# A decoder layer whose shared expert moves from first to last in the feed-forward order

## The chip, the core and the metric

The kernel runs on one core of a Trainium2 chip. A core has five engines with queues of their own: TensorE (PE in the profile, its weight loads PEld), VectorE (DVE), ScalarE (ACT), GpSimd (POOL) and SyncE (SP, which here only starts transfers). They meet through semaphores that the program sets and waits for. The metric is the device time of one execution in microseconds (us). Smaller is better.

## The reference, cut to what matters

One decoder layer on 8 sequences of 56 tokens and 128 channels: self-attention with 16 heads, attention over a context of 1500 rows by random features, and a feed-forward part with one shared expert and eight routed experts. Each part is added to its input. The change touches the feed-forward part:

```python
def _L0_ffn_ref(x, W_router, W_up, W_down, W_sh_up, W_sh_down):
    logits = x_flat @ W_router
    probs = jax.nn.sigmoid(logits)
    topk_probs, topk_idx = jax.lax.top_k(probs, TOPK)
    topk_probs = topk_probs / (jnp.sum(topk_probs, axis=-1, keepdims=True) + 1e-06)
    combine = jnp.zeros((N, E), dtype=x.dtype).at[jnp.arange(N)[:, None], topk_idx].add(topk_probs)
    out = sq_relu(x_flat @ W_sh_up) @ W_sh_down
    for e in range(E):
        h = sq_relu(x_flat @ W_up[e])
        out = out + combine[:, e:e + 1] * (h @ W_down[e])
```

All eight routed experts are computed for all 448 tokens; the combine weights are zero for those that a token did not choose. Each expert has 512 hidden columns, and `sq_relu` is the square of the positive part.

## The kernel before, in words

The program is written out by hand, one list of instructions for each engine; nothing reorders them. The 8 sequences go as 4 pairs (`PAIRS`). The attention of a pair and the context products of two sequences alternate up to 64 us of the profiled execution. From there the last pair's second half (residual, norm, context attention, norm) is a chain of small steps across four engines, into which TensorE puts feed-forward products of the first three pairs. After that only feed-forward work is left.

The hidden columns of the nine experts are 36 chunks of 128 (`NCH`), `c` = 0 to 35, four to an expert. Before, chunks 0 to 3 are the shared expert and chunks 32 to 35 the last routed one. The first 32 (`NSP`) are computed with each operand split into a high half in float32r and a low half, three products for each result: high by high, low weights by high, high weights by low. The last four are plain float32 products. For each chunk:

- TensorE makes the up product (`up`, 3 matmuls of 448 columns) into one of five banks, five chunks ahead of the down product (`down`, 3 more) into one of the output banks, of which before has two (C0, K0), in turn by expert.
- ScalarE takes the positive part (`relu`), and later the high half of the squared result (`hidden_high`, to `hh`); for some early chunks it also squares (`square`). VectorE squares the others (`hidden`).
- The low half `hl` is the square less `hh` (`hidden_low`): GpSimd does it for chunks with `on_pool(c)`, VectorE for the others. The down product of a chunk ends with the one that reads `hl`.
- When an expert's four down products are there, VectorE multiplies the bank by the expert's row of combine weights (`expert_out`), and GpSimd adds the product to the running sum `acc` (`add_expert`).

The combine weights go a long way: router products for each pair (`router`), exponent on ScalarE, `choose_probs` to `choose_weights` on VectorE, four small transposes on TensorE into X0, a copy to `cT` on ScalarE, a write to memory (`share`) by SyncE and reads of it that spread each expert's row over 128 partitions (`cb`). `s_cb[0]` counts the first two rows, `s_cb[1]` the rest.

The down weights arrive in six pieces of six chunks (`weights(k)`, k = 6 to 11), ScalarE takes their high halves (`weights_high`) and GpSimd their low ones (`weights_low`). For the late pieces the tables `LATE_AT` and `LOW_AT` say after which chunk each is done. On GpSimd, then, low halves of the hidden values, low halves of weights and the additions of experts stand in one queue. At chunk c it does `hidden_low(c)`, then `add_expert` (where c ends an expert), then `weights_low`.

At the end the last chunk's products stand in C0, the sum `acc` is transposed into X0, VectorE adds X0 to the residual `x2` (`base`), then multiplies C0 by the last expert's combine weight and adds, a pair at a time (`fin`, four operations). Two transfers of two pairs each leave from SyncE's and ScalarE's queues. `keep_warm(n)` is n float32 products of 128 columns with no use but to keep TensorE busy.

## Time and profile before

| | us |
|---|---|
| Runs of the kernel | 126.13 median (124.91, 126.13, 127.34) |
| The profiled execution's own time | 124.76 |
| Its span, first to last instruction | 123.0 |
| TensorE busy | 113.9 (93%) |
| VectorE busy | 89.6 (73%) |
| ScalarE busy | 75.8 (62%) |
| GpSimd busy | 59.1 (48%) |

Busy times overlap between engines. The share of TensorE counts every matmul from its start to its modelled end, so neighbours overlap; where only one stage matters, start-to-start distances are the ones to read. The profiled execution lies below all three timed runs. Feed-forward work fills the stretch from about 72.5 us to 119.5 us.

### The profile page before, as it was taken

The numbers are of one execution on the slowest core, as the hardware profiler recorded it, in microseconds if no ns is written. First come the engines' busy times: TensorE is split into PE (matmuls) and PEld (weight loads), VectorE is DVE, ScalarE is ACT, GpSimd is POOL, SyncE is SP. The second block draws the span as 40 slices with busy tenths as digits, with TensorE's granted clock in tenths as the row PEclk, the third lists the DMA queues.
The fourth block names the chain that finished last, engine by engine and source line by source line (L and its number), as shares of the span: only waits on it lengthen the run. The fifth ranks groups of instructions, "written<-read, shape, count | busy, mean of one in ns | idle before, by whom it ended". The sixth has DMA issues, their size and how long they took to land.

```text
span 123.0 us, 3129 instructions
## 1 busy us (share of the span) xinstructions
PE 113.9 (93%) x1171; PEld 91.1 (74%) x1171; DVE 89.6 (73%) x241; ACT 75.8 (62%) x167; POOL 59.1 (48%) x65
## 2 busy tenths in 40 slices
PE   3989999999999999999996969999999999999980
PEld 2357757686869676776674859989998999999980
DVE  0679898227969686967664469999579999999442
ACT  4013527983677566871941766999768988986300
POOL 6397242351965289251011041637957794673110
PEclk9999999999999999999999996799999999999999
DMA  3899999769969995992000000032892000000002
GB/s 117 236 316 374 406 426 392 248 247 290 351 185 424 344 419 142 418 347 80 0 5 0 0 3 0 5 53 87 241 303 101 3 0 0 5 0 0 0 0 85
DMA packets 6198, 20.46 MB, mean 166 GB/s; under 512 B 776, under 2 KB 2344, under 8 KB 6184
## 3 DMA queue, kind: packets, MB, share of 16 engines
q1 hardware_dynamic: 6040, 20.14, 46.3%
q8 instruction: 9, 0.15, 0.5%
q10 hardware_dynamic: 144, 0.13, 0.3%
q14 instruction: 5, 0.04, 0.1%
HBM read 19.99 MB, written 0.28 MB: 165 GB/s over the span
## 4 chain that ended last, share of the span: by engine, by line
PE 85%; DVE 6%; POOL 4%; issue 2%; ACT 1%; DVEq 0%; POOLq 0%
PE RA L378 6%; PE K L304 5%; PE C L293 5%; PE K L440 3%; PE C L556 3%; PE C L646 3%; PE C L553 3%; PE RA L331 3%; PE C L552 3%; PE K L556 3%; PE K L552 3%; PE K L553 3%; PE RA L552 3%; PE M L402 3%; PE RA L556 3%; PE RB L388 2%
## 5 line engine op out<-in xcount | busy, mean ns | idle before, releaser
L881 POOL TENSOR_TENSOR hl<-craw,hh 128x448 fp32r<-128x448 f32 (+2 forms) x12 | 12.9, 1073 | 12.8 <-ACT hh L799 12.8
L845 POOL TENSOR_TENSOR rstd<-vpe,mhalf 128x1 f32<-128x1 f32 (+1 forms) x10 | 5.8, 583 | 23.5 <-DVE vpe L980 23.5
L881 POOL TENSOR_TENSOR wul<-wraw,wuh 128x768 fp32r<-128x768 f32 x6 | 10.9, 1822 | 8.4 <-ACT wuh L693 8.4
L881 POOL TENSOR_TENSOR wdl<-wraw,wdh 128x768 fp32r<-128x768 f32 (+1 forms) x6 | 9.9, 1653 | 3.3 <-ACT wdh L693 3.3
L926 POOL TENSOR_TENSOR kT<-kT,qT 128x448 f32<-128x448 f32 x7 | 8.1, 1152 | 5.8 <-DVE qT L1261 5.8
L785 ACT ACTIVATE rt<-RA 128x448 f32<-128x448 f32 (+2 forms) x17 | 8.5, 498 | 1.2 <-PE RA L556 0.9
L799 ACT ACTIVATE hh<-craw 128x448 fp32r<-128x448 f32 (+2 forms) x16 | 7.9, 503 | 1.3 <-DVE craw L1222 1.2
L785 ACT ACTIVATE rt<-RB 128x448 f32<-128x448 f32 (+2 forms) x15 | 7.7, 517 | 0.7 <-PE RB L556 0.7
L378 PEld LDWEIGHTS RA<-kT,qT 64*64 64x64 f32 x256 | 7.1, 134 | 0.8 <-issue 0.8
L378 PE MATMUL RA<-kT,qT 64*64 64x56 f32 x256 | 7.6, 221 | 0.0
L965 DVE STREAM_TRANSPOSE rft<-rf 128x384 f32<-128x384 f32 x8 | 4.6, 575 | 3.5 <-ACT rf L684 3.4
L293 PE MATMUL C<-craw,pk 128*32 128x384 f32 x64 | 6.7, 492 | 0.4 <-ACT rf L684 0.4
L304 PE MATMUL K<-craw,rft 128*32 128x129 f32 x192 | 6.9, 277 | 0.0
L556 PE MATMUL C<-hl,wdh 128*128 128x448 f32 (+2 forms) x19 | 6.9, 365 | 0.0
L553 PE MATMUL C<-hh,wdl 128*128 128x448 f32 (+2 forms) x19 | 6.8, 360 | 0.0
L552 PE MATMUL C<-hh,wdh 128*128 128x448 f32 (+2 forms) x19 | 6.7, 352 | 0.0
L552 PE MATMUL RA<-y3h,wuh 128*128 128x448 f32 (+2 forms) x17 | 6.4, 377 | 0.0
L873 POOL TENSOR_TENSOR ktok<-rt 128x256 f32<-128x256 f32 x8 | 5.7, 730 | 1.4 <-DVE rt L1035 1.4
L684 ACT ACTIVATE rf<-C 128x384 f32<-128x384 f32 x8 | 3.9, 490 | 3.5 <-PE C L293 3.3
L553 PE MATMUL RA<-y3h,wul 128*128 128x448 f32 (+2 forms) x17 | 6.0, 356 | 0.0
L552 PE MATMUL K<-hh,wdh 128*128 128x448 f32 x16 | 6.0, 372 | 0.0
L556 PE MATMUL K<-hl,wdh 128*128 128x448 f32 x16 | 5.9, 368 | 0.0
(185 smaller groups left out, 338.1 us busy)
## 6 DMA issues: line engine op xcount, KB each, us to landing
craw<-ctx_nat SPq DMA_DIRECT2D x8, 780.0 KB, 6.2
craw<-ctx_tr SPq DMA_DIRECT2D x8, 768.0 KB, 5.7
wraw<-w_up SPq DMA_DIRECT2D x6, 384.0 KB, 6.2
wraw<-w_down SPq DMA_DIRECT2D x5, 384.0 KB, 3.4
craw<-share SPq DMA_DIRECT2D x7, 224.0 KB, 4.3
pk<-pack SPq DMA_DIRECT2D x1, 388.0 KB, 4.9
pk<-pack SPq DMA_DIRECT2D x1, 256.0 KB, 2.8
wde<-w_down SPq DMA_DIRECT2D x1, 256.0 KB, 6.5
```

The source lines that it names most:

```text
L293: mm = pe.matmul(C0[M * g:M * (g + 1), 0:GL], col("proj"), ctxtv[:, b % RING, g, :], start=True, stop=True)
L304: mm = pe.matmul(K0[M * g:M * (g + 1), 0:D + 1], rft[:, b % 2, j, :], tiles(b)[:, j, 0:D + 1], start=(j < GR), stop=(j >= CT - GR))
L378: mm = pe.matmul(RA[i * SLOT:(i + 1) * SLOT, o, j * T:(j + 1) * T], qT[r, j, i * SLOT:(i + 1) * SLOT], kT[r, j, i * SLOT:i * SLOT + T], st ...
L552: pe.matmul(bank, wh, xh, start=first, stop=False)
L553: pe.matmul(bank, wl, xh, start=False, stop=False)
L556: return pe.matmul(bank, wh, xl, start=False, stop=last)
L785: act.activation(rl[n % 2][:, t], ubank[c % UB][:, t], ACT.Relu).then_inc(S["rl"], 1)
L799: act.activation(hh[:, c % 4, t], full(c, t), ACT.Copy).then_inc(S["hh"], 1)
L845: pool.tensor_tensor(dst, src, mhalf[:, 0:src.shape[1]], ALU.pow).then_inc(S[done], 1)
L873: pool.tensor_tensor(ktok[:, heads_g, HD:QK], rt[0][:, heads_g, :], rt[1][:, heads_g, :], ALU.add).then_inc(S["kadd"], 1)
L881: pool.tensor_tensor(dst, src, high.bitcast(F32), ALU.subtract).then_inc(S[done], 1)
L926: pool.tensor_tensor(accv, accv, ot[:, e % 2, :].rearrange("p (b t) -> p b t", b=B), ALU.add).then_inc(S["accp"], 1)
```

## The change

The shared expert becomes the last of nine. Its four chunks are 32 to 35 (plain float32), and the eight routed experts are chunks 0 to 31. So:

- Its result needs no weight, and the end has no multiply. Its products add straight onto the transposed sum and the residual in two banks, X0 (pairs 2 and 3) and C0 (pairs 0 and 1). The residual of pairs 2 and 3 comes in by a product with the identity, the sum by products with the identity in place of transposes. ScalarE copies X0's half out and VectorE adds the residual to C0's half.
- Expert 0 is now routed: its bank is multiplied by `cb[0]` after chunk 11, expert 1 after chunk 13. There are three output banks (C0, K0, X0).
- The turning of the combine weights on TensorE stands after chunk 4 instead of 3.
- GpSimd's chunks are 1, 5 and 7 of eight instead of 1, 3 and 7, and `LATE_AT` and `LOW_AT` change.
- SyncE starts piece 10 of the weights after the reads of `share`, of which there are eight instead of seven.
- The routers of the first three pairs move ahead of `y2_transpose(3)`, all four up products too; the warming products are 1, 5 and 2 in three waits instead of 2 in one.

```diff
-LATE_AT = (8, 13, 21)
-LOW_AT = (5, 8, 13, 21)
+LATE_AT = (8, 14, 21)
+LOW_AT = (8, 11, 14, 21)
-WARM_Y3 = 2
+WARM_Y3, WARM_GATE = 5, 2
...
-        obank = [C0[:, :], K0[:, :]]
+        obank = [C0[:, :], K0[:, :], X0[:, :]]
+        lbank = [C0[:, :], X0[:, :]]
...
-            return c % 8 in (1, 3, 7) and c < NSP - 1
+            return c % 8 in (1, 5, 7) and c < NSP - 1
...
-            for e in range(E - 1):
+            for e in range(E):
                 sp.dma_start(cb[:, e, :], share[e:e + 1, :, :].rearrange("e b t -> e (b t)").broadcast_to([128, NT])).then_inc(s_cb[e > 1], 16)
             weights(k)
+            weights(k + 1)
...
-            for c in range(3):
+            for c in range(4):
                 up_high(c, 0, done)
+            pe.wait_ge(S["x1"], PAIRS)
+            for q in range(p):
+                router(q)
             y2_transpose(p)
-            up_high(3, 0, done)
+            pe.wait_ge(S["kvs"], B)
+            keep_warm(1)
             query_features(p)
...
-            for q in range(p):
-                router(q)
             down_high(0)
             keep_warm(WARM_Y3)
             y3_transpose(p)
+            keep_warm(WARM_GATE)
...
                 if k == 0:
-                    pe.wait_ge(S["ot"], E - 2)
+                    pe.wait_ge(S["ot"], 5)
+                    pe.matmul(X0[:, 256:512], ident, x2[:, 2:4, :].rearrange("p q d -> p (q d)"), start=True, stop=False)
...
-                for p in range(PAIRS):
-                    mm = pe.transpose(X0[:, p * 128:(p + 1) * 128], acc[:, 2 * p:2 * p + 2, :].rearrange("p b t -> p (b t)"), ident)
-                mm.then_inc(S["ftp"], 1)
+                for p in (2, 3, 0, 1):
+                    pe.matmul(lbank[p // 2][:, p * 128:(p + 1) * 128], acc[:, 2 * p:2 * p + 2, :].rearrange("p b t -> p (b t)"), ident,
+                              start=False, stop=False)
...
-                if c == 3:
+                if c == 4:
                     pe.wait_ge(S["cmb"], 1)
...
-            act.wait_ge(S["fin"], PAIRS)
+            act.wait_ge(S["dl"], 1)
+            act.activation(fin[:, 2:4, :], X0[:, 256:512].rearrange("p (q d) -> p q d", q=2), ACT.Copy).then_inc(S["fin2"], 1)
+            act.wait_ge(S["fin2"], 1)
             act.dma_start(out[:, 2:4, :], fin[:, 2:4, :]).then_inc(s_out, 16)
...
                 v.wait_ge(S["dn"], CHUNKS * (e + 1))
+                v.wait_ge(s_cb[e > 1], 16 * (2 if e <= 1 else E - 2))
                 if e == 0:
-                    step(v.tensor_copy(accv, tok(obank[0][:, 0:NT])), "acc0")
+                    step(v.tensor_tensor(accv, tok(obank[0][:, 0:NT]), tok(cb[:, 0, :]), ALU.mult), "acc0")
                     return
...
-                step(v.tensor_tensor(ot[:, e % 2, :], obank[e % 2][:, 0:NT], cb[:, e - 1, :], ALU.mult), "ot")
+                step(v.tensor_tensor(ot[:, e % 2, :], obank[e % 3][:, 0:NT], cb[:, e, :], ALU.mult), "ot")
...
-                if c % CHUNKS == CHUNKS - 1 and CHUNKS < c < NCH - 1:
+                if c in (11, 13):
+                    expert_out((c - 11) // 2)
+                if c % CHUNKS == CHUNKS - 1 and 11 < c < NCH - 1:
                     expert_out(c // CHUNKS - 1)
...
-            v.wait_ge(S["ftp"], 1)
-            step(v.tensor_tensor(x2[:, :, :], X0[:, :].rearrange("p (q d) -> p q d", q=PAIRS), x2[:, :, :], ALU.add), "base")
-            own("base")
             v.wait_ge(S["dn"], NCH)
-            for p in range(PAIRS):
-                step(v.scalar_tensor_tensor(out=fin[:, p, :], in0=obank[E % 2][:, p * 128:(p + 1) * 128],
-                                            scalar=sel[:, 4, p, E - 1:E], in1=x2[:, p, :], op0=ALU.mult, op1=ALU.add), "fin")
+            step(v.tensor_tensor(fin[:, 0:2, :], C0[:, 0:256].rearrange("p (q d) -> p q d", q=2), x2[:, 0:2, :], ALU.add), "fin")
```

The first place is GpSimd's queue in the feed-forward part. `hl` rows are low halves of hidden values, `wdl` rows low halves of down weights, and `kT<-kT,qT` rows are `add_expert` (the sum lies in `kT`, an expert's product in `qT`). Before, from piece 8 on (chunks 5 to 17):

```order
L881 TENSOR_TENSOR wdl<-wraw,wdh 128x768 [waits s_wh]
L881 TENSOR_TENSOR hl<-craw,hh 128x448 [waits s_dn,s_hh]
L881 TENSOR_TENSOR wdl<-wraw,wdh 128x768 [waits s_wh]
L881 TENSOR_TENSOR hl<-craw,hh 128x448 [waits s_dn,s_hh] x2
L926 TENSOR_TENSOR kT<-kT,qT 128x8x56 [waits s_acc0,s_ot]
L881 TENSOR_TENSOR wdl<-wraw,wdh 128x768 [waits s_wh]
L881 TENSOR_TENSOR hl<-craw,hh 128x448 [waits s_dn,s_hh]
L926 TENSOR_TENSOR kT<-kT,qT 128x8x56 [waits s_accp,s_ot]
L881 TENSOR_TENSOR hl<-craw,hh 128x448 [waits s_dn,s_hh] x2
```


In the changed kernel, from piece 8 (chunks 8 to 15):

```order
L896 TENSOR_TENSOR wdl<-wraw,wdh 128x768 [waits s_wh]
L896 TENSOR_TENSOR hl<-craw,hh 128x448 [waits s_dn,s_hh]
L941 TENSOR_TENSOR kT<-kT,qT 128x8x56 [waits s_acc0,s_ot]
L896 TENSOR_TENSOR wdl<-wraw,wdh 128x768 [waits s_wh]
L896 TENSOR_TENSOR hl<-craw,hh 128x448 [waits s_dn,s_hh]
L896 TENSOR_TENSOR wdl<-wraw,wdh 128x768 [waits s_wh]
L896 TENSOR_TENSOR hl<-craw,hh 128x448 [waits s_dn,s_hh]
L941 TENSOR_TENSOR kT<-kT,qT 128x8x56 [waits s_accp,s_ot]
```


Piece 9 now stands behind the first addition of an expert, and the low half of chunk 13 behind both; then piece 10 and the low half of chunk 15.

The second place is VectorE around the wait for the combine rows (`s_cb0`). `craw` holds hidden values as well as the combine rows, and `qT<-K,craw` is the product of an expert with its row. Before, chunks 11 to 13:

```order
L958 TENSOR_TENSOR hl<-RA,hh 128x448 [waits s_dn,s_hh]
L1261 TENSOR_TENSOR qT<-K,craw 128x448 [waits s_cb0,s_dn]
L1222 SCALAR_TENSOR_TENSOR RB<-RB,rt 128x448 [waits s_rl] x2
L958 TENSOR_TENSOR hl<-RB,hh 128x448 [waits s_dn,s_hh]
L1222 SCALAR_TENSOR_TENSOR M<-M,rt 128x448 [waits s_rl]
L958 TENSOR_TENSOR hl<-RB,hh 128x448 [waits s_dn,s_hh]
```


In the changed kernel, chunks 11 to 13 (`kT<-C,craw` is expert 0):

```order
L973 TENSOR_TENSOR hl<-RA,hh 128x448 [waits s_dn,s_hh]
L1272 TENSOR_TENSOR kT<-C,craw 128x8x56 [waits s_cb0,s_dn]
L1237 SCALAR_TENSOR_TENSOR RB<-RB,rt 128x448 [waits s_rl]
L973 TENSOR_TENSOR hl<-RA,hh 128x448 [waits s_dn,s_hh]
L1237 SCALAR_TENSOR_TENSOR craw<-RB,rt 128x448 [waits s_hlp,s_hh,s_rl]
L973 TENSOR_TENSOR hl<-RB,hh 128x448 [waits s_dn,s_hh]
L1276 TENSOR_TENSOR qT<-K,craw 128x448 [waits s_cb0,s_dn]
```


The product that feeds GpSimd's first addition was the first operation behind the wait. Now it is the sixth.

The third place is TensorE's end, chunks 32 to 35. Before:

```order
L646 MATMUL C<-wde,craw 128x128 [waits s_h,s_wde,s_ot]
L646 MATMUL C<-wde,craw 128x128 x3
L646 MATMUL C<-wde,craw 128x128 [waits s_h]
L646 MATMUL C<-wde,craw 128x128 x3
L646 MATMUL C<-wde,craw 128x128 [waits s_h]
L646 MATMUL C<-wde,craw 128x128 x3
L654 MATMUL X<-pk,kT 128x128 [waits s_accp]
L654 MATMUL X<-pk,kT 128x128 x3
L646 MATMUL C<-wde,craw 128x128 [waits s_h]
L646 MATMUL C<-wde,craw 128x128 x3
```


In the changed kernel, from chunk 33 on:

```order
L657 MATMUL X<-wde,craw 128x128 [waits s_h]
L657 MATMUL X<-wde,craw 128x128
L657 MATMUL C<-wde,craw 128x128 x2
L657 MATMUL X<-wde,craw 128x128 [waits s_h]
L657 MATMUL X<-wde,craw 128x128
L657 MATMUL C<-wde,craw 128x128 x2
L667 MATMUL X<-pk,kT 128x128 [waits s_accp]
L667 MATMUL X<-pk,kT 128x128
L667 MATMUL C<-pk,kT 128x128 x2
L657 MATMUL X<-wde,craw 128x128 [waits s_h]
L657 MATMUL X<-wde,craw 128x128
L657 MATMUL C<-wde,craw 128x128 x2
```


Each chunk now does pairs 2 and 3 first, into X0, and the four transposes are products (`L667`, without a count of their own). The product of the residual with the identity, 256 columns, stands ahead of chunk 32.

## Rows read from the trace of the kernel before

**Rows 1.** The page's busy times: engine, us, share of the span, instructions.

```profile
PE 113.9 (93%) x1171; PEld 91.1 (74%) x1171; DVE 89.6 (73%) x241; ACT 75.8 (62%) x167; POOL 59.1 (48%) x65
```

**Rows 2.** Busy time by stretch: length, five engines, TensorE's granted clock, DMA share, GB/s.

```profile
75.00:78.00 3.00, 3.00 (x11) 2.83 (x11) 2.85 (x25) 2.26 (x7) 0.43 (x1) 0.50 0.00 0
...
74.50:78.50 4.00, 4.00 (x17) 3.77 (x16) 3.64 (x28) 3.20 (x9) 0.85 (x2) 0.57 0.02 4
...
122.00:123.00 1.00, 0.00 (x0) 0.00 (x0) 0.00 (x0) 0.00 (x0) 0.00 (x0) 0.75 0.11 35
```

**Rows 3.** TensorE's waits, 66 to 72.6 us: who waited for whom, total, times, longest.

```profile
PE X L418 <- DVE y L983: 1.1, 1, 1.1
...
PE X L435 <- DVE y L983: 0.6, 1, 0.6
...
PE M L582 <- ACT y3h L675: 0.5, 1, 0.5
```

**Rows 4.** TensorE in order of time: start, length, work; low products of chunks 13 and 15.

```profile
93.19 0.43 PE L556 MATMUL K<-hl,wdh 128*128 128x448 f32 x1
...
95.71 0.37 PE L556 MATMUL K<-hl,wdh 128*128 128x448 f32 x1
```

**Rows 5.** ScalarE in order of time: first after its last gap, and the combine copy.

```profile
76.14 0.30 ACT L799 ACTIVATE hh<-craw 128x112 fp32r<-128x112 f32 x1 [0.65 <-DVE craw L1222]
...
82.06 0.59 ACT L675 ACTIVATE kT<-X 8x512 f32<-8x512 f32 x1
```

**Rows 6.** SyncE's queue in order of time: the write of share and its reads.

```profile
82.68 0.83 SPq L271 DMA_DIRECT2D share<-kT  x1
...
84.89 3.19 SPq L274 DMA_DIRECT2D craw<-share  x7
```

**Rows 7.** VectorE in order of time.

```profile
79.31 1.77 DVE L1300 TENSOR_TENSOR sel<-sel 128x32 f32<-128x32 f32 x1
...
88.99 0.62 DVE L1261 TENSOR_TENSOR qT<-K,craw 128x448 f32<-128x448 f32 x1 [1.32 <-DMA craw<-share]
...
89.53 1.15 DVE L1222 SCALAR_TENSOR_TENSOR RB<-RB,rt 128x448 f32<-128x448 f32 x2
```

**Rows 8.** GpSimd in order of time.

```profile
79.19 1.84 POOL L881 TENSOR_TENSOR wdl<-wraw,wdh 128x768 fp32r<-128x768 f32 x1
...
84.74 1.85 POOL L881 TENSOR_TENSOR wdl<-wraw,wdh 128x768 fp32r<-128x768 f32 x1
...
86.55 1.16 POOL L881 TENSOR_TENSOR hl<-craw,hh 128x448 fp32r<-128x448 f32 x1
...
94.31 1.15 POOL L881 TENSOR_TENSOR hl<-craw,hh 128x448 fp32r<-128x448 f32 x1 [0.91 <-ACT hh L799]
...
95.43 1.15 POOL L926 TENSOR_TENSOR kT<-kT,qT 128x448 f32<-128x448 f32 x1
```

**Rows 9.** All engines at the end, in order of time.

```profile
115.36 2.84 PE L646 MATMUL C<-wde,craw 128*128 128x128 f32 x24
...
118.03 0.60 PE L654 MATMUL X<-pk,kT 128*128 128x128 f32 x4
...
118.47 1.06 PE L646 MATMUL C<-wde,craw 128*128 128x128 f32 x8
...
118.67 0.69 DVE L1317 TENSOR_TENSOR x<-X,x 128x512 f32<-128x512 f32 x1 [1.43 <-PE X L654]
...
119.64 1.13 DVE L1321 SCALAR_TENSOR_TENSOR y<-C,sel,x 128x128 f32<-128x128 f32 x4 [0.28 <-PE C L646]
...
120.28 0.34 SPq L278 DMA_DIRECT2D out<-y  x1
...
120.80 0.37 ACTq L832 DMA_DIRECT2D out<-y  x1
```

**Rows 10.** TensorE in order of time: three routers, two warming products.

```profile
69.38 0.73 PE L582 MATMUL M<-pk,y3T 128*128 128x8 f32 x6
...
70.40 0.61 PE L311 MATMUL K<-pk 128*128 128x128 f32 x4
```

More of the change, by code:

```diff
@@ L264, in _ @@
                 context_n(b)
-                for _ in range((0, 2, 0, 2, 1, 2, 1, 3)[b]):
+                for _ in range((0, 2, 0, 2, 1, 2, 1, 2)[b]):
                     weights(k)
                     k += 1
-            assert k == 2 * NPC - 1
+            assert k == 2 * NPC - 2
             sp.wait_ge(S["cT"], 1)
@@ L586, in down_high @@
                 e, j = divmod(c, CHUNKS)
-                if j == 0 and e >= 2:
-                    pe.wait_ge(S["acc0"], 1) if e == 2 else pe.wait_ge(S["ot"], e - 2)
+                if j == 0 and e == 2:
+                    pe.wait_ge(S["cT"], 1)
+                if j == 0 and e >= 3:
+                    pe.wait_ge(S["acc0"], 1) if e == 3 else pe.wait_ge(S["ot"], e - 3)
                 if c % PIECE == 0:
@@ L641, in down_last @@
                 if k == 0:
-                    pe.wait_ge(S["ot"], E - 2)
+                    pe.wait_ge(S["ot"], 5)
+                    pe.matmul(X0[:, 256:512], ident, x2[:, 2:4, :].rearrange("p q d -> p (q d)"), start=True, stop=False)
                     pe.wait_ge(s_wde, 16)
                 pe.wait_ge(S["h"], products(nth(c)))
-                for p in range(PAIRS):
-                    mm = pe.matmul(obank[E % 2][:, p * 128:(p + 1) * 128],
+                for p in (2, 3, 0, 1):
+                    if k == 0 and p == 0:
+                        pe.wait_ge(S["ot"], 6)
+                    mm = pe.matmul(lbank[p // 2][:, p * 128:(p + 1) * 128],
                                    he[:, k, 2 * p:2 * p + 2, :].rearrange("p b t -> p (b t)"), wde[:, k, :],
-                                   start=(k == 0 and p == 0), stop=(k == CHUNKS - 1 and p == PAIRS - 1))
+                                   start=(k == 0 and p == 0), stop=(k == CHUNKS - 1 and p % 2 == 1))
+                    if k == CHUNKS - 1 and p == 3:
+                        mm.then_inc(S["dl"], 1)
                 mm.then_inc(S["dn"], 1)
@@ L691, in weights_high @@
             def weights_high(k):
-                act.wait_ge(s_w[k % 2], 16 * (k // 2 + 1))
+                act.wait_ge(s_w[k % 2], 16 * (k // 2 + 1 + (k >= NPC - 1 and k % 2)))
                 act.activation((wuh if k < NPC else wdh)[:, pieces(k), :], raw(k), ACT.Copy).then_inc(S["wh"], 1)
```

20 lines of the change are left out of this document (10 added, 10 removed).

## The prediction, made before the changed kernel ran

> **What bounds the kernel now.** I read the page's busy times first: TensorE is busy for 113.9 of 123.0 us [rows 1]. That is an average, so I went to TensorE in order of time. From about 78 us to the last product it never stands still for more than a few tenths: the low products of chunks 13 and 15 start at 93.19 and 95.71 us, and that is 2.52 us for two chunks [rows 4]. Any matmul added there, and any late operand, goes straight onto the end.
>
> Three other things are to be seen. The clock: in the four microseconds from 74.5 the granted clock is 0.57 on average, and from 75 to 78 it is 0.50, the lower level of 1.2 GHz [rows 2]. At 0.57, 0.43 x 4.0 = 1.7 us of full-speed time are lost, so the low stretch is 3.4 us long. TensorE had waited 1.1, 0.6 and 0.5 us a little before [rows 3]. Second, the combine rows: VectorE reaches the first product with them and waits until 88.99 us [rows 7] for reads that SyncE began at 84.89 [rows 6]. Third, the end: after the last product VectorE works from 119.64 to 120.77, and the last transfer is issued at 120.80 [rows 9], 2.2 us before the end.
>
> **The change, part by part.**
>
> *Routers and warming products.* Three routers are six instructions, 0.73 us [rows 10], and two warming products are four, at 0.111 each by the end's rows [rows 9, 10]. The moved routers fit the 1.1 us wait, and the 1, 5 and 2 warming products (0.22, 1.1 and 0.44 us) fit waits that the chain of small steps sets anyway [rows 3], so they cost nothing. If that cover were gone they would cost 0.7 and 1.8 us. They gain nothing by themselves either: the wait ends when the small steps end. What they can bring is the clock, between 0 and 1.7 us [rows 2]. I take it that the early fall does go away, since each of the three waits is filled for the most part.
>
> *Where that gain ends.* ScalarE runs without a gap from 76.14 us to the copy of the combine weights at 82.06 [rows 5]; a faster TensorE moves this by perhaps 0.2 us. VectorE has 1.77 us on an operation on 32 columns at 79.31, which ends with the GpSimd operation that began at 79.19 [rows 7, 8]. GpSimd is empty there now, so the weights are chosen about 1.5 us sooner, and turning them a chunk later does not hold the copy. The write and reads of `share` then follow as before, 82.68 and 84.89 less 0.2 [rows 6], and the first two rows land at about 88.8 instead of 88.99. So whatever TensorE gained before chunk 11 it has to give back there: the low half of chunk 11 now stands on VectorE behind the wait, third in line, and ends at 88.8 + 2 x 0.54 + 0.6 = 90.5 us. An operation on VectorE starts 0.54 us after the one before (88.99 to 89.53 [rows 7]). I count the clock gain as 0 from chunk 11 on.
>
> *GpSimd's queue.* This is the largest term. The product that GpSimd's first addition waits for is sixth behind the combine rows: 88.8 + 5 x 0.54 = 91.5, ending at 92.1. Behind it GpSimd has the addition (1.12 us from start to start by its neighbour at 94.31 to 95.43), piece 9 (84.74 to 86.55, 1.81 us), and then the low half of chunk 13 (1.15) [rows 8]. With 0.1 us for the semaphore, that is 92.2 + 1.12 + 1.81 + 1.15 = 96.3 us. TensorE read it at 93.19 [rows 4]: 3.1 us late. Then piece 10 (1.81) and the low half of chunk 15 (1.15) end at 99.2, where TensorE stood at 95.71: 3.5 us late. TensorE's own work between the two is only 2.5 us, so it waits again, by about 0.5. The next addition and chunk 17's low half are ready at 101.5, just when TensorE comes, so the delay stops there. Term: +3.5. From below: if the product were first behind the rows as before, 2.7 sooner, the same queue would end chunk 15 at 96.5, 0.8 late. From above: the early fall of the clock remains and the copy of the weights, a chunk later, slips 0.9; then +4.4. I take 3.5, nearest to the rows of the wait itself. By the lengths of the rows in place of the start distances the first sum is 0.1 longer. The Trainium skill says under Perfetto Trace Analysis, GPSIMD Engine Instruction, that a GpSimd span in a profile is unreliable and that one should go by start-to-start spacing; that favours the value taken, and the trace agrees, 1.81 against 1.85.
>
> *SyncE.* It passes one wait fewer before the write of `share`, and piece 10 now starts behind eight reads of 0.46 us each (seven took 3.19 [rows 6]), at about 88.3 us. ScalarE needs it at chunk 14 and would wait until perhaps 95 us; the hidden values of chunks 14 and 15 are then ready before 97.5, ahead of GpSimd's 99.2. Hidden, cost 0; were GpSimd's queue not late, this would cost 1 to 2 us by itself.
>
> *TensorE's end.* Twenty-four instructions of 128 columns take 118.03 - 115.36 = 2.67 us, 0.111 each, and a float32 product is two of them; the four transposes are one each, 0.44 us together [rows 9]. As products they cost 8 x 0.111 = 0.88, so +0.44. The product of 256 columns costs two instructions of 256, taken as twice 0.22: +0.44. Sum +0.88, all on the path. The Trainium skill says in TensorE: Matmul & The Clock Gate, Terms, that transpose mode is 4 times faster for float32. By that rule the four products would cost 1.76 us, the sum would be 1.76 in place of 0.88, and the time about 130.1 us; the rows here show a factor of 2.
>
> *The finish.* Four operations from 119.64 to 120.77 become one on 256 columns, between 0.35 (one on 128 columns) and 0.69 (the one on 512) [rows 9]; I take 0.45. The 128x512 addition was already beside TensorE's work, so its removal gives nothing. ScalarE's copy of the other half begins 0.44 us sooner, two products before the last, and is no later. So the last issue comes 0.57 us after the last product instead of 1.27: -0.70, bounds -0.80 and -0.46.
>
> *A second fall of the clock.* TensorE would stand still from about 93.0 to 96.3 us. In the last microsecond of the profile, 122 to 123, the granted clock averages 0.75 [rows 2], so it fell at about 122.5, 3.0 us after the last product. So I expect it to fall here. For 3.4 us TensorE would run at half speed, but partly while it waits for GpSimd anyway: from 96.3, the low product, an up product, chunk 14 and an up and a high product take until 100.1 instead of 98.7, against GpSimd's 99.2. Term +0.8, between 0 and 1.7.
>
> Sum: 3.5 + 0.88 - 0.70 + 0.8 = 4.5 us on the profiled execution's 124.76, **129.2 us**. The median of the runs, 126.13, is 1.4 above that execution; by that offset it would be 130.6, in the range, but slow stretches in the part that now waits would be hidden, so I keep 129.2.
>
> **The rivals.**
>
> *A, a shorter queue, chance 0.20.* The combine rows land sooner or VectorE clears the queue faster, and chunk 15 is 1 to 2.2 us late (from 0.8, the bound above, to halfway); no second fall. 124.76 + 0.18 + 1.0 to 2.2 = 125.9 to 127.1. For it: one weight piece fewer goes out just ahead of the write. Against: the write took 2.2 us and the first reads 4.1, and nothing in the change shortens either.
>
> *B, the clock gain is kept, chance 0.12.* The other side. The clock stays up and no operand is late: 124.76 - 1.7 + 0.18 = 123.2. It decides from the point where the rows land 7.4 us (96.3 - 88.8 - 0.1) before TensorE reads chunk 13's low half, at 93.19 - 1.7 = 91.5: that is 84.1 us, before the reads are even issued. Only if the queues' prices differ from these rows can this be.
>
> *C, the clock falls as before and the queue is late, chance 0.15.* The filled waits leave the falling edge where it was, since the short products of the last pair, just before it, are unchanged. Then +4.4 - 0.1 + 0.18 + 0.8: 130.0.
>
> *D, nothing but the end changes, chance 0.08.* The clock as before and the queue hidden: 124.76 + 0.18 = 124.9.
>
> **How the numbers follow.** My forecast has 0.45: 129.2, or 128.4 without the second fall (0.10 of the 0.45). About 2% is what a measurement of this kernel can tell from no change, 123.6 to 128.65. Faster is B, 0.12. Same is A, D and the forecast without the second fall, 0.20 + 0.08 + 0.10 = 0.38. Slower is the rest of the forecast and C, 0.35 + 0.15 = 0.50. The range of 124.5 to 131.5 takes in A, D, C and the forecast with its bounds, the full 1.7 of a second fall among them, and leaves out B and a little of C.
>
> **What would show it.** In the changed profile: no granted clock below 1 from 74 to 79; the combine rows landing between 88.5 and 89; GpSimd's first addition at 92.2, followed without a gap by a 768-column weight piece; a wait of TensorE of about 3 us at chunk 13 and 0.5 at chunk 15; a granted clock near 0.5 after it; at the end eight instructions in 0.88 us where four took 0.44, and the last issue 0.6 us after the last product. I am wrong if the rows land before 87 us, or if GpSimd reaches chunk 13's low half before 93.

## The result, and the profile after

The changed kernel takes 129.72 us (median of 4 runs, 129.59 to 130.1), the kernel before 125.64 beside it. The ratio is 1.0386 (1.0346 to 1.0426): slower by 4%. Forecast was 129.2 in a range of 124.5 to 131.5. Here and below, a ratio leaves out executions in a slower state of the chip, a median does not. The profiled execution took 130.1 us with a span of 128.3. The page's busy times, for [rows 1]:

```profile
PE 116.5 (91%) x1189; PEld 92.2 (72%) x1189; DVE 85.4 (67%) x237; ACT 75.7 (59%) x168; POOL 58.8 (46%) x65
```

TensorE is 2.6 us busier in a span 5.3 us longer, so 2.7 us of the difference are idle time of TensorE.

Two executions must first be laid over each other. In the stretch before 62 us the change moves nothing but one weight transfer, which it splits in two (tested below), and yet the two differ there. The last product of the context values ahead of the last pair's chain of small steps starts, in TensorE's order of time, in the kernel before at

```profile
60.68 0.44 PE L429 MATMUL X<-kvs,rfq 128*64 128x129 f32 x4
```

and in the changed kernel at

```profile
62.80 0.44 PE L433 MATMUL X<-kvs,rfq 128*64 128x129 f32 x4
```

ScalarE, in order of time, shows where most of it was lost, waiting for a piece of the up weights (before, the same wait was 0.37 us):

```profile
39.94 0.84 ACT L706 ACTIVATE wuh<-wraw 128x768 fp32r<-128x768 f32 x1 [2.29 <-DMA wraw<-w_up]
```

So 2.1 us of the profiled difference arise before the changed work. All that follows is compared by its distance from this product, called **t0**.

**The clock.** Busy time by stretch of the changed kernel:

```profile
74.00:79.00 5.00, 4.91 (x37) 4.64 (x36) 4.23 (x23) 3.63 (x14) 1.33 (x2) 1.00 0.02 5
...
96.00:102.00 6.00, 3.78 (x17) 3.19 (x18) 3.92 (x7) 4.84 (x11) 6.00 (x6) 1.00 0.22 68
```

The early fall of [rows 2] is gone, 1.00 from 74 to 79. The second fall that I forecast is not in this execution. But its three other timed runs had a mean granted clock of 0.987 over their spans of 127.8 to 128.0: 0.013 x 128 = 1.7 us of full-speed time lost.

**TensorE's waits.** The view of waits of the changed kernel (who waited for whom, total, times, longest):

```profile
PE C L560 <- POOL hl L896: 3.2, 2, 3.0
```

TensorE in order of time, low products of chunks 13 and 15, for [rows 4] (in brackets the idle time before it and what ended it):

```profile
98.00 0.47 PE L560 MATMUL C<-hl,wdh 128*128 128x448 f32 x1 [2.98 <-POOL hl L896]
...
100.92 0.47 PE L560 MATMUL C<-hl,wdh 128*128 128x448 f32 x1 [0.22 <-POOL hl L896]
```

Chunk 13 stands at t0 + 35.20 (before 93.19 - 60.68 = 32.51), chunk 15 at t0 + 38.12 (before 35.03): 2.7 and 3.1 us late.

**VectorE and GpSimd.** VectorE in order of time, for [rows 7]: the choice of the weights, the first product with the combine rows, the second.

```profile
81.08 0.19 DVE L1318 TENSOR_TENSOR sel<-sel,tden 128x32 f32<-128x32 f32 x1
...
90.59 0.62 DVE L1272 TENSOR_TENSOR kT<-C,craw 128x448 f32<-128x448 f32 x1 [1.22 <-DMA craw<-share]
...
93.26 0.61 DVE L1276 TENSOR_TENSOR qT<-K,craw 128x448 f32<-128x448 f32 x1
```

GpSimd in order of time, for [rows 8]:

```profile
93.95 1.15 POOL L941 TENSOR_TENSOR kT<-kT,qT 128x448 f32<-128x448 f32 x1 [4.56 <-DVE qT L1276]
95.05 1.80 POOL L896 TENSOR_TENSOR wdl<-wraw,wdh 128x768 fp32r<-128x768 f32 x1
96.81 1.14 POOL L896 TENSOR_TENSOR hl<-craw,hh 128x448 fp32r<-128x448 f32 x1
97.90 1.85 POOL L896 TENSOR_TENSOR wdl<-wraw,wdh 128x768 fp32r<-128x768 f32 x1
99.71 1.15 POOL L896 TENSOR_TENSOR hl<-craw,hh 128x448 fp32r<-128x448 f32 x1
```

TensorE in order of time, the turning of the combine weights:

```profile
83.14 0.60 PE L680 MATMUL X<-pk,sel 128*8 128x128 f32 x4
```

The weights are chosen at 81.27, but TensorE comes to the turning only at 83.14 (t0 + 20.34, before t0 + 20.75), right behind chunk 4: in the changed kernel it is TensorE's own pace that sets the turning. The combine rows let VectorE go at 90.59, t0 + 27.79 (before 28.31). The product for GpSimd's first addition is sixth, five places of 0.53 us later, and ends at 93.87. From there GpSimd works without a gap: addition, piece 9, low half 13, piece 10, low half 15. TensorE takes chunk 13 when the third of these ends.

**SyncE and ScalarE.** SyncE's queue in order of time, for [rows 6]:

```profile
84.39 0.83 SPq L274 DMA_DIRECT2D share<-kT  x1
86.59 3.66 SPq L277 DMA_DIRECT2D craw<-share  x8
90.29 6.92 SPq L257 DMA_DIRECT2D wraw<-w_down  x2
```

ScalarE in order of time: the high half of piece 10, and of chunk 14's hidden values.

```profile
96.64 0.84 ACT L706 ACTIVATE wdh<-wraw 128x768 fp32r<-128x768 f32 x1 [3.22 <-DMA wraw<-w_down]
...
97.81 0.54 ACT L812 ACTIVATE hh<-M 128x448 fp32r<-128x448 f32 x1
```

Piece 10 is the first of the two transfers at 90.29, and ScalarE stands still 3.22 us for it. The hidden value of chunk 14 is ready at 98.35; TensorE wants it at 98.92, after its own late chunk 13.

**The end**, for [rows 9]. TensorE in order of time, residual's product first:

```profile
120.64 0.59 PE L651 MATMUL X<-x,pk 128*128 128x256 f32 x2
121.07 0.61 PE L657 MATMUL X<-wde,craw 128*128 128x128 f32 x4
...
123.75 0.61 PE L667 MATMUL X<-pk,kT 128*128 128x128 f32 x4
124.19 0.61 PE L667 MATMUL C<-pk,kT 128*128 128x128 f32 x4
...
125.09 0.61 PE L657 MATMUL C<-wde,craw 128*128 128x128 f32 x4
```

ScalarE and its queue:

```profile
125.29 0.39 ACT L845 ACTIVATE y<-X 128x256 f32<-128x256 f32 x1 [4.52 <-PE X L657]
125.70 0.37 ACTq L847 DMA_DIRECT2D out<-y  x1
```

VectorE:

```profile
125.73 0.42 DVE L1334 TENSOR_TENSOR y<-C,x 128x256 f32<-128x256 f32 x1 [3.21 <-PE C L657]
```

SyncE's queue:

```profile
126.19 0.34 SPq L282 DMA_DIRECT2D out<-y  x1
```

From the residual's product to the last end: 125.70 - 120.64 = 5.06 us. Before, 115.36 to the end of the last product (119.53) was 4.17. The last issue is 0.49 us after the last product (before 1.27).

### The profile page after: what moved, and what is told of

Its sections match the earlier page's. It is cut to its first block, busy times and chain, and to the rows that moved or that the text cites. A ratio compares the mean times of both kernels' runs of the same rounds, so it can differ in the third digit from the quotient of the medians.

```text
span 128.3 us, 3165 instructions
## 1 busy us (share of the span) xinstructions
PE 116.5 (91%) x1189; PEld 92.2 (72%) x1189; DVE 85.4 (67%) x237; ACT 75.7 (59%) x168; POOL 58.8 (46%) x65
## 4 chain that ended last, share of the span: by engine, by line
PE 54%; ACT 10%; POOL 10%; issue 9%; DMA 9%; DVE 7%; SPq 0%; POOLq 0%; ACTq 0%; DVEq 0%
PE RA L382 4%; DMA wraw<-w_up 4%; PE K L308 4%; PE K L444 3%; PE C L297 3%; PE RB L343 3%; POOL wul L896 3%; DMA craw<-share 3%; ACT hh L812 2%; POOL hl L896 2%; DMA share<-kT 2%; PE C L560 2%; PE RB L348 1%; PE C L657 1%; PE X L657 1%
## 5 line engine op out<-in xcount | busy, mean ns | idle before, releaser
L560 PE MATMUL C<-hl,wdh 128*128 128x448 f32 (+2 forms) x15 | 5.3, 355 | 3.2 <-POOL hl L896 3.2
L706 ACT ACTIVATE wdh<-wraw 128x768 fp32r<-128x768 f32 (+1 forms) x6 | 4.6, 766 | 3.5 <-DMA wraw<-w_down 3.5
L343 PE MATMUL RB<-pk,yT 128*128 128x256 f32 x16 | 5.1, 449 | 1.3 <-ACT kT L688 1.3
L706 ACT ACTIVATE wuh<-wraw 128x768 fp32r<-128x768 f32 x6 | 4.9, 836 | 2.3 <-DMA wraw<-w_up 2.3
L998 DVE TENSOR_SCALAR y<-x,mv,rstd 128x128 f32<-128x128 f32 x8 | 2.8, 344 | 5.0 <-POOL rstd L860 5.0
```

The lines of the kernel that those rows point to most:

```text
L343: mm = pe.matmul(key_heads(g)[:, :, HD:QK], yT[:, p, :], col("krope")[:, g * 256:(g + 1) * 256], start=True, stop=True)
L560: return pe.matmul(bank, wh, xl, start=False, stop=last)
L706: act.activation((wuh if k < NPC else wdh)[:, pieces(k), :], raw(k), ACT.Copy).then_inc(S["wh"], 1)
```

## The experiments

"Aligned end" below is the span less t0 of the profiled execution: 62.3 us before, 65.5 for the changed kernel. Each batch has its own runs of the kernel before. The expectations stand word for word.

**The kernel before once more**, to see how steady t0 is.

> The kernel before once more, unchanged, for a second trace. Question: is the 2.1 us by which the changed kernel's trace lags already at the last context products (62.80 against 60.68 us) the change's, or does the time up to there vary from execution to execution? Theory V (it varies): the same instruction lies 0.5 us or more from 60.68, and a piece of the up weights lands later. Theory S (the split transfer of piece 5 in the changed kernel does it): it lies within 0.3 us of 60.68.

It took 124.74 us with t0 at 60.54 and an aligned end of 62.4. By its own test that spoke for theory S, the split; the next run and the second trace of the changed kernel (t0 at 61.32 with the split) speak against it. VectorE had chosen the combine weights at t0 + 18.9 here, against t0 + 20.6 in the first trace, and the turning (t0 + 20.8) and the rows (t0 + 28.4) came no sooner for it.

**The layout of the weights.** The changed kernel splits one weight transfer in two, since the shared expert's weights lie first in memory. Here they lie last, and the splitting goes.

```diff
-                sp.dma_start(raw(k)[:, 0:b - a, :], src[:, a + CHUNKS:b + CHUNKS, :]).then_inc(s_w[k % 2], 16)
-                if k == NPC - 1:
-                    sp.dma_start(raw(k)[:, b - a:PIECE, :], src[:, 0:CHUNKS, :]).then_inc(s_w[k % 2], 16)
+                sp.dma_start(raw(k), src[:, pieces(k), :]).then_inc(s_w[k % 2], 16)
...
```

> The changed kernel, with both weight arrays laid out in memory in the new order of experts, so that piece 5 of the up weights is one transfer again. Theory S (the split holds up ScalarE at piece 4, 2.3 us of waiting in the trace): about 1.5 us faster than 129.7, so 128.2, and TensorE's wait of 1.26 us at 41.8 us is gone. Theory V (chance of that execution, not the split): 129.7 within 0.3, since all four runs of the changed kernel lie within 0.5 us.

TensorE in order of time, t0:

```profile
61.86 0.44 PE L431 MATMUL X<-kvs,rfq 128*64 128x129 f32 x4
```

Four runs of 128.34 to 135.28 us, median 130.56, too scattered for a ratio or for either theory's number. In the traces of this study whose transfer is split, t0 was 62.80, 61.32, 60.62, 61.95, 61.31 and 61.94 (and 68.60 in one with further falls of the clock before t0, the old front below); without the split, 61.86 here and 61.98 in the best end of the change below; in the kernel before and its variants, 60.5 to 61.7. So the split does not explain 62.80, and t0 varies by 2 us from run to run. What makes it vary was not found.

**GpSimd's order.** Low half 13 first, then the addition, then piece 9.

```diff
-LOW_AT = (8, 11, 14, 21)
+LOW_AT = (8, 13, 14, 21)
...
-                if c % CHUNKS == CHUNKS - 1 and c >= 3 * CHUNKS - 1:
+                if c == 13:
+                    add_expert(1)
+                if c % CHUNKS == CHUNKS - 1 and c > 3 * CHUNKS:
```

> The changed kernel with GpSimd's queue turned round at one place: the low half of chunk 13 first, then the first addition, then piece 9. Theory G (the wait at chunk 13 is GpSimd's queue, and piece 10, for which ScalarE waits 3.2 us, stands right behind it): chunk 13's low product starts about 3 us sooner, but chunk 14 then waits for ScalarE, whose high half of chunk 14 ends at 98.3 in the trace of the changed kernel against 98.9 when TensorE wanted it: 0.4 to 0.8 us faster, about 129.1. Rival H (the transfer's wait costs nothing, as I summed): 2.5 to 3.1 us faster, about 126.9. Rival N (the wait is for something else): no change.

TensorE in order of time, the first high product of chunk 14:

```profile
96.39 0.47 PE L556 MATMUL C<-hh,wdh 128*128 128x448 f32 x1 [2.40 <-ACT hh L812]
```

ScalarE in order of time, the high half of piece 10:

```profile
94.62 0.84 ACT L706 ACTIVATE wdh<-wraw 128x768 fp32r<-128x768 f32 x1 [3.06 <-DMA wraw<-w_down]
```

129.02 us, ratio to before 1.0307 (1.0192 to 1.0422); the gain of 0.70 us is within the scatter of its runs (128.12 to 130.03). The wait for GpSimd is gone, and one of 2.40 us for ScalarE stands a chunk later, because ScalarE waits for piece 10: theory G. The clock fell again in this trace (mean 0.987), and the aligned end is 66.7 us, 0.5 less than the changed kernel's 67.2 with a fall (its second trace, below). Two waits lay side by side, and mending one uncovers the other.

**Piece 10 later**, at chunk 17 in place of 14, GpSimd's order as in the change.

```diff
-LATE_AT = (8, 14, 21)
-LOW_AT = (8, 11, 14, 21)
+LATE_AT = (8, 17, 21)
+LOW_AT = (8, 11, 17, 21)
```

> The changed kernel with piece 10 of the weights taken by ScalarE and GpSimd at chunk 17 instead of 14, nothing else. Theory G: the wait of 3.0 us at chunk 13 stays, since addition and piece 9 still stand ahead of its low half; only the short wait at chunk 15 (0.2 to 0.4 us) goes: 129.3. Rival T (the late transfer is what holds the chain): 2 us faster or more, 127.5.

TensorE in order of time, the low product of chunk 13:

```profile
97.17 0.47 PE L560 MATMUL C<-hl,wdh 128*128 128x448 f32 x1 [3.00 <-POOL hl L896]
```

GpSimd in order of time, behind piece 9:

```profile
95.99 2.23 POOL L896 TENSOR_TENSOR hl<-craw,hh 128x448 fp32r<-128x448 f32 x2
```

128.95 us, ratio 1.0292 (1.0213 to 1.0371). The wait at chunk 13 is as long as ever, 3.00 us, as theory G has it. GpSimd now takes the low halves of 13 and 15 one behind the other, so only the second wait is gone; the aligned end is 65.05 us against 65.5, neither with a fall of the clock.

**Both**, and piece 9 at chunk 9.

```diff
-LATE_AT = (8, 14, 21)
-LOW_AT = (8, 11, 14, 21)
+LATE_AT = (8, 17, 21)
+LOW_AT = (8, 9, 17, 21)
...
-                if c % CHUNKS == CHUNKS - 1 and c >= 3 * CHUNKS - 1:
+                if c == 13:
+                    add_expert(1)
+                if c % CHUNKS == CHUNKS - 1 and c > 3 * CHUNKS:
```

> The changed kernel with both queues eased: GpSimd makes the low half of chunk 13 ahead of the first addition, makes piece 9 after chunk 9 (where it stood idle 4.6 us), and piece 10 is taken by ScalarE and GpSimd at chunk 17. Theory G (the loss at chunks 13 to 15 is these two queues, either of which hides the other): no wait of TensorE over 0.6 us after 74 us, the granted clock stays up, 3.5 to 4.5 us faster than 129.7: 125.2 to 126.2. Rival K (the combine rows themselves hold the chain, and VectorE's six operations behind them become the next wait): 127.5 or more.

TensorE's waits, the longest from t0 on:

```profile
PE K L560 <- POOL hl L896: 0.5, 1, 0.5
```

125.67 us, ratio 1.0035 (1.0 to 1.0071). By the medians the two edits gave 0.70 and 0.77 us alone, and with piece 9 moved as well they give 4.05; what piece 9 adds was not run by itself. The longest wait of TensorE after t0 is 0.5 us, and the mean clock was 0.999 or 1.0 in 9 of 10 runs, where 3 of 4 runs of the changed kernel had 0.987. So up to 1.7 of the 4.05 us are the second fall of the clock, which comes no more. The aligned end is 63.5 us, 2.0 less than the changed kernel's without a fall. It is still 1.2 more than before's 62.3, though the medians are only 0.4 apart. TensorE in order of time, the low product of chunk 17:

```profile
99.81 0.47 PE L560 MATMUL K<-hl,wdh 128*128 128x448 f32 x1 [0.54 <-POOL hl L896]
```

Chunk 15's stands at t0 + 34.88 (before 35.03), this one at t0 + 38.50 (before 37.46): most of what is left of the loss is here, where piece 10 is now taken.

**The end by itself.** No product for the residual; VectorE adds it to both halves.

```diff
-                    pe.matmul(X0[:, 256:512], ident, x2[:, 2:4, :].rearrange("p q d -> p (q d)"), start=True, stop=False)
...
-            act.activation(fin[:, 2:4, :], X0[:, 256:512].rearrange("p (q d) -> p q d", q=2), ACT.Copy).then_inc(S["fin2"], 1)
...
+            step(v.tensor_tensor(fin[:, 2:4, :], X0[:, 256:512].rearrange("p (q d) -> p q d", q=2), x2[:, 2:4, :], ALU.add), "fin2")
```

> The changed kernel with another end alone: no product of the residual with the identity; VectorE adds the residual to both halves, the first while TensorE finishes the second. Theory E (the 256-column product is 0.44 us on the path, as two 0.11 instructions per 128 columns): 0.4 us faster, about 129.3, and the last issue stays 0.5 us after the last product. Rival: the first half's addition (0.42 us) holds up the second, and nothing is gained: 129.7.

VectorE in order of time, the last two operations:

```profile
125.38 0.42 DVE L1331 TENSOR_TENSOR y<-X,x 128x256 f32<-128x256 f32 x1 [2.33 <-PE X L656]
125.83 0.42 DVE L1333 TENSOR_TENSOR y<-C,x 128x256 f32<-128x256 f32 x1
```

SyncE's queue, the last issue:

```profile
126.28 0.34 SPq L282 DMA_DIRECT2D out<-y  x1
```

TensorE's end takes 125.79 - 121.17 = 4.62 us in place of 5.06, and the last issue is again 0.49 us after the last product: the product cost 0.44 and nothing takes its place. The time was 128.99 us, ratio 1.027 (1.0169 to 1.0371). Its run at a clock of 1.0 took 127.36, the three at 0.985 to 0.987 took 128.75, 129.24 and 130.23; with t0 varying by 2 us, such times alone don't price a fall of the clock.

**The old routers and warming** (the old front) in the changed kernel.

```diff
-WARM_Y3, WARM_GATE = 5, 2
+WARM_Y3, WARM_GATE = 2, 0
...
-            for c in range(4):
+            for c in range(3):
...
-            pe.wait_ge(S["x1"], PAIRS)
-            for q in range(p):
-                router(q)
-            pe.wait_ge(S["kvs"], B)
-            keep_warm(1)
+            up_high(3, 0, done)
...
+            pe.wait_ge(S["kvs"], B)
...
+            for q in range(p):
+                router(q)
...
-            keep_warm(WARM_GATE)
```

> The changed kernel with the routers and warming products where the kernel before has them. Theory A (what the clock gives ahead of chunk 11 is taken back at the combine rows): the granted clock falls to 0.5 for 3.4 us near 75 us again, and the time is 129.7 to 130.6, since only the copy of the weights slips. Rival L (the gain of the clock is kept to the end): 1.7 us slower, 131.4. If the clock does not fall, the 11 us of warming were not what kept it.

TensorE in order of time, t0 and the turning of the combine weights:

```profile
68.60 0.44 PE L433 MATMUL X<-kvs,rfq 128*64 128x129 f32 x4
...
92.11 0.60 PE L678 MATMUL X<-pk,sel 128*8 128x128 f32 x4
```

VectorE in order of time, the first product with the combine rows, and busy time by stretch:

```profile
99.55 0.62 DVE L1270 TENSOR_TENSOR kT<-C,craw 128x448 f32<-128x448 f32 x1 [1.20 <-DMA craw<-share]
...
81.00:87.00 6.00, 6.00 (x25) 5.87 (x25) 4.30 (x28) 2.64 (x11) 1.19 (x2) 0.50 0.00 0
80.00:88.00 8.00, 7.60 (x33) 7.43 (x33) 5.02 (x31) 4.64 (x16) 1.33 (x2) 0.57 0.01 2
```

Six runs of 130.81 to 140.21 us, median 132.96, ratio 1.0517 (1.0403 to 1.0631). Its two runs with the fewest falls (mean clock 0.974: 0.026 x 130 = 3.4 us lost, two falls) took 130.81 and 131.48, near rival L and above theory A; the changed kernel's with one fall took 129.59 to 129.77. Since t0 varies by as much as that difference, the trace has to decide. It has further falls before t0, and an early fall twice as long as before's: 0.43 x 8 = 3.4 us of full-speed time lost. From t0 it shows where they go. The turning stands at t0 + 23.51 against 20.34 in the changed kernel, the rows at t0 + 30.95 against 27.79, chunk 13's low product at t0 + 38.35 against 35.20, and the aligned end is 69.8 against 67.2, each with a second fall behind chunk 13. So 3.2 of the 3.4 us reach the rows and 2.6 the end: rival L, and not theory A. Nothing was taken back at the combine rows.

**The new routers and warming** (the new front) in the kernel before.

```diff
-WARM_Y3 = 2
+WARM_Y3, WARM_GATE = 5, 2
...
-            for c in range(3):
+            for c in range(4):
                 up_high(c, 0, done)
+            pe.wait_ge(S["x1"], PAIRS)
+            for q in range(p):
+                router(q)
             y2_transpose(p)
-            up_high(3, 0, done)
+            pe.wait_ge(S["kvs"], B)
+            keep_warm(1)
...
-            pe.wait_ge(S["kvs"], B)
-            for q in range(p):
-                router(q)
+            keep_warm(WARM_GATE)
```

> The kernel before with the changed kernel's routers and warming products alone. The granted clock stays at 1 from 74 to 79 us. Theory A: TensorE gains up to 1.7 us on chunks 3 to 8, but in the trace of before the low halves of chunks 13 and 15 end at 93.1 and 95.5 us, 0.1 and 0.3 us before TensorE reads them, and what makes them hangs on the combine rows: at most 0.3 us faster, 125.1. Rival L (kept): 1.7 us faster, 123.7.

TensorE's waits, the longest from t0 on:

```profile
PE X L669 <- DVE sel L1305: 1.2, 1, 1.2
```

124.79 us, ratio 0.9965 (0.9924 to 1.0006), clock 0.994 or more. The early fall is gone, and a wait of 1.2 us for the chosen weights has come at the turning. The aligned end is 62.1 against 62.3. Of the 1.7 us of clock, 0.2 reach the end in this trace. The kernel before itself says the same. Its clock doesn't fall early in every execution: of its 49 runs beside the experiments, 18 have a mean clock of 0.999 or 1.0 and 22 one of 0.980 to 0.986, and their medians are 124.9 and 125.2 us. With the new front and no long wait behind it (this kernel, "both" above and the last three below) 46 of 48 runs have 0.994 or more, so the front does keep the clock.

**The changed kernel once more.**

> The changed kernel, unaltered, for a second profiled execution. In the first one the granted clock stood at 1.0 throughout, while its other timed runs averaged 0.987 over the span. Theory F (a second fall of the clock after the wait at chunk 13 is the rule, and the first profiled execution missed it by chance, while 2.1 us of its time were lost before 62 us by chance as well): about 129.7 us, the product before the last pair's chain between 60.6 and 62, a wait of about 3.0 us at chunk 13's low product, and a granted clock near 0.72 over the six microseconds after it, 1.7 us lost. Rival N (the fall belongs to no particular place): clock of 1.0 again, or a fall elsewhere. If product and clock both do well, 128.0 us; if both do badly, 131.4.

TensorE in order of time, the low product of chunk 13:

```profile
96.53 0.47 PE L560 MATMUL C<-hl,wdh 128*128 128x448 f32 x1 [2.97 <-POOL hl L896]
```

Busy time by stretch:

```profile
98.00:102.00 4.00, 3.92 (x13) 3.30 (x12) 3.75 (x8) 3.14 (x7) 3.88 (x4) 0.57 0.02 5
96.00:102.00 6.00, 5.40 (x17) 4.27 (x18) 4.66 (x9) 5.14 (x11) 5.65 (x5) 0.72 0.24 67
```

130.3 us, t0 at 61.32. The wait is 2.97 us, chunk 13 stands at t0 + 35.21 as in the first trace, and then the granted clock is 0.57 for four microseconds: 0.43 x 4 = 1.7 us lost at the lower level, 1.2 GHz. The aligned end is 67.2 = 65.5 + 1.7: theory F. TensorE in order of time, the last low product (chunk 31), in the first trace of the changed kernel and in this one:

```profile
120.44 0.36 PE L560 MATMUL K<-hl,wdh 128*128 128x448 f32 x1
```

```profile
120.60 0.37 PE L560 MATMUL K<-hl,wdh 128*128 128x448 f32 x1
```

That is t0 + 57.64 and t0 + 59.28, 1.64 later with the fall. Two more traces had the fall and the same work up to there: the layout's stands at t0 + 58.85 and that of the end by itself at t0 + 59.03, 1.2 and 1.4 later, though each lost 1.7 us of full-speed time too (0.21 x 8, from 96 to 104). So part of a fall can be hidden.

**The best end of the change**: the reordered queues, the layout, VectorE's two additions together (their diffs stand above).

> The changed kernel with the reordered queues (GpSimd takes chunk 13's low half first, then its first addition; piece 9 at chunk 9, piece 10 at chunk 17) and with the end in which no product brings in the residual and VectorE adds it to both halves; the pieces of the weights lie in memory so that piece 11 comes in one transfer. Terms: reordered queues 125.67 in their own run, the end -0.44 to -0.55, the layout 0. Theory S (the change has nothing left but its end, and that can be made as short as before's): 125.2 us, the same as the kernel before within 0.5. Rival: with the queues mended the kept clock shows and the kernel is faster than before by 1 us or more, 124.3 or less.

125.06 us against 124.98, ratio 0.9997 (0.997 to 1.0023). The forecast of "the same" holds; the kept clock brings nothing beyond before.

**The kernel before, with the new front and two banks for its last chunk's products.**

```diff
...
+        lbank = [C0[:, :], RA[:, 1, :]]
...
-                    mm = pe.matmul(obank[E % 2][:, p * 128:(p + 1) * 128],
+                    mm = pe.matmul(lbank[p // 2][:, p * 128:(p + 1) * 128],
...
-            v.wait_ge(S["dn"], NCH)
+            v.wait_ge(S["dl"], 1)
...
+                if p == 2:
+                    v.wait_ge(S["dn"], NCH)
```

> The kernel before (shared expert first) with two things: the routers and warming products placed as in the changed kernel, and the last chunk's products in two banks, so that VectorE works on pairs 0 and 1 while TensorE does pairs 2 and 3. Terms: the first alone gave 124.79; the second takes two of VectorE's four last operations (0.28 us each by their starts) off the end, -0.55. Theory: 124.2 us, 1.1 below the kernel before. Rival: the end is set by the transfer on ScalarE's queue, which is no sooner, 124.8.

VectorE in order of time, the sum with the residual and the four last operations:

```profile
118.72 0.69 DVE L1322 TENSOR_TENSOR x<-X,x 128x512 f32<-128x512 f32 x1 [1.43 <-PE X L659]
119.45 0.61 DVE L1328 SCALAR_TENSOR_TENSOR y<-C,sel,x 128x128 f32<-128x128 f32 x2
119.97 0.60 DVE L1328 SCALAR_TENSOR_TENSOR y<-RA,sel,x 128x128 f32<-128x128 f32 x2
```

124.57 us, ratio 0.995 (0.9913 to 0.9987): the fastest version, half a per cent below before, and not to be told from the new front alone (ratio 0.9965). The forecast was 124.2. VectorE's addition of the sum now holds it until 119.41, so pairs 0 and 1 begin only 0.13 us before TensorE is done (119.58), and the last issue, 120.61, is 1.03 us after the last product against 1.27: 0.24 gained in place of 0.55.

**The turning at chunk 4 in that kernel.**

```diff
-                if c == 3:
+                if c == 4:
```

> The kernel of the run before it in this batch, with the combine weights turned on TensorE after chunk 4 in place of 3; nothing else. With the routers moved, TensorE waited 1.2 us for the chosen weights at the turning. Theory A (the end is set by the combine rows and the GpSimd queue behind them, so that time saved before them is given back): the 1.2 us go, but a wait of about the same size appears at chunks 11 to 15; gain 0 to 0.2 us, 124.0 to 124.3. Rival K (kept): about 1 us faster, 123.2, and no new wait after chunk 10.

TensorE in order of time, chunk 4's low product:

```profile
81.76 0.47 PE L557 MATMUL K<-hl,wdh 128*128 128x448 f32 x1 [1.18 <-DVE hl L963]
```

VectorE in order of time, the first product with the combine rows:

```profile
90.24 0.63 DVE L1266 TENSOR_TENSOR qT<-K,craw 128x448 f32<-128x448 f32 x1 [1.34 <-DMA craw<-share]
```

126.11 us, ratio 1.0084 (1.0043 to 1.0124): 1.5 slower than the run before it, and both theories missed. The wait did not move to chunks 11 to 15. It turned into one of 1.18 us at chunk 4's low half, which VectorE makes right behind the choice of the weights, so the turning came 1.45 us later from t0. The combine rows followed (29.52 us after t0 against 28.11, +1.41), and so did the end (63.2 against 61.8, +1.4).

## Why the prediction was right, and where it was not

The total was right, and so was the mechanism of the loss, GpSimd's queue. One step, where the gain of the clock ends, was right in its number for the wrong reason, and some sizes were off. By steps, with t0 taken off:

- **Routers and warming products cost nothing: right.** The last router starts at t0 + 11.76 (74.56 us), before at t0 + 11.80 (72.48).
- **The early clock fall goes away: right.** It is gone in both traces of the changed kernel. That the kernel before has it only in part of its executions I had not seen.
- **Its gain ends at the combine rows: right for the kernel before, wrong for the changed one.** The new front alone brought 124.79 against 125.26, 0.2 us by the trace: there TensorE stands 1.2 us at the turning, until VectorE has chosen the weights. In the changed kernel the weights are chosen 1.9 us before TensorE comes to the turning, so the chain through the rows hangs on TensorE's pace. I had hung it on ScalarE, "a faster TensorE moves this by perhaps 0.2 us". Taking the clock away delayed the rows by 3.2 us for 3.4 us lost (one trace, the old front), where my sum had 0 and my case C 0.9 for half such a loss. The forecast number held, rows 0.5 us sooner from t0 than before and 0.2 forecast, because the clock's gain was spent on turning the weights a chunk (1.2 us) later. The one-line move of the turning shows that a delay of the rows reaches the end in the kernel before too, 1.41 us at the rows and 1.4 at the end.
- **GpSimd's queue, +3.5: right in kind, 0.4 too large.** Chunk 15 is 3.1 us late and chunk 13 2.7 (3.1 forecast). The order and the prices held: 93.95 to 97.90 is 1.10 + 1.76 + 1.09 = 3.95 us for addition, piece 9 and low half 13, against 4.08 in my sum. The rest is the rows' 0.3 us. The Trainium skill, Perfetto Trace Analysis, GPSIMD Engine Instruction, calls GpSimd's spans unreliable and goes by start-to-start spacing; here each span is 0.04 to 0.05 us longer than the spacing, so it agrees, and is worth 0.1 in the sum.
- **SyncE and piece 10, cost 0: right by 0.6 us, and too small by itself.** ScalarE's value was ready 0.57 us before TensorE wanted it. Uncovered, the wait was 2.40 us, and I had written 1 to 2. This is the step whose size mattered most for whoever mends the kernel: mending GpSimd alone gave 0.70 by the medians and 0.5 by the traces. Starting piece 10 ahead of the reads of `share`, as before, is the plainest way to take this wait off, and it was not run.
- **TensorE's end, +0.88: measured +0.89.** The four products are 0.44 us each pair, eight instructions in 0.89 (123.75 to 124.64), where before four took 0.44. With the factor of 4 for float32 that the Trainium skill gives (TensorE: Matmul & The Clock Gate, Terms) an estimate for them is 1.76 us; the trace shows a factor of 2. The residual's product cost 0.43, and taking it away gave 0.44.
- **The finish, -0.70: measured -0.87.** The last issue is 0.49 us after the last product, not 0.57, and the rest is 0.1 less between last issue and end (2.1 against 2.2).
- **The second fall, +0.8, between 0 and 1.7: the size was off.** It came in 3 of the 4 runs and in the second trace, where 1.6 to 1.7 us of the 1.7 lost reach the end. I had half of it hidden behind GpSimd; TensorE waited only 0.22 us for chunk 15 in the first trace, so there was little to hide behind. In the two other traces with the same work it cost 1.2 and 1.4. By its terms the trace with the fall is 3.1 + 0.89 - 0.87 + 1.7 = 4.8 above before from t0 (measured 67.2 - 62.3 = 4.9), the one without it 3.1 (measured 3.2); I had 4.5.

The total came within 0.5 us partly by luck. The queue was 0.4 too large and the finish 0.2, the fall 0.4 to 0.8 too small, and the sum stood on the one profiled execution of the kernel before, 0.9 below its median. The first profiled execution came near it by more luck: no second fall, and 2.1 us lost before t0 that I had not looked for. Of rivals, the sooner queue (A) and the kept clock (B) are out by these rows, and so is C, since the early fall is gone. "Nothing but the end" (D) is about what the reordered queues give, 125.67 measured, 124.9 forecast.

## What to carry to other kernels

When work moves behind a late arrival, lay out the queue of every engine that stands behind it, in order and with start-to-start prices: that gave the 3 us here from rows of the kernel before. Look then for a second wait under the first, because mending one of two parallel waits gave 0.7 us, and both together, with the fall of the clock that followed them, 4.05. And ask of a saved microsecond which engine comes last at the next meeting point. At the turning of the combine weights it was VectorE in the kernel before, once the clock was kept, and a faster TensorE gained next to nothing; in the changed kernel it was TensorE, and 3.2 of 3.4 us lost ahead of the turning reached the rows.

## What the runs showed of the chip that was not expected

- The same stretch of work before t0, the same instructions and transfers, took 60.5 to 62.8 us in different executions (68.6 in one with further falls of the clock). ScalarE's wait for a piece of up weights was 2.29 us in the changed kernel's first trace and 0.54 in its second.
- After a wait of 2.40 to 2.98 us the granted clock fell to its lower level of 1.2 GHz in some executions and not in others, with waits of the same length (2.98 and 3.00 without, 2.97 and 2.98 with, the last in the old front's trace). It then took 1.7 us of full-speed time each time, of which 1.2 to 1.6 us stood at the last low product.
- VectorE's operation on 32 columns took 1.77 us beside a GpSimd operation [rows 7, 8] and 0.20 where GpSimd was idle (VectorE of the changed kernel, in order of time):

```profile
80.85 0.20 DVE L1315 TENSOR_TENSOR sel<-sel 128x32 f32<-128x32 f32 x1
```

  The Trainium skill (SBUF — State Buffer, SBUF: two separate sides) says that a VectorE operation with two SBUF inputs and a GpSimd operation that reads SBUF lock each other out for the whole instruction. The trace agrees: in the kernel before it ends with GpSimd's at 81.0. In the second trace of that kernel the same operation began at 78.22, just ahead of GpSimd's at 78.26, and took 0.19 us, and the next one on 32 columns, behind GpSimd's start, took 1.03. The weights were chosen at t0 + 18.5 in the changed kernel (81.27) and t0 + 20.6 before (81.30), and the turning, a chunk later, gave none of it to the rows.
